# Six PSUM banks and exponentials of 1024 columns in the last two groups of an attention and experts kernel

## The reference

```python
scores = jnp.einsum('bsqhd,bthd->bqhst', qh, kh) * scale
probs = jax.nn.softmax(scores, axis=-1)
a_dot = jnp.einsum('bqhst,bthd->bsqhd', probs, vh)
...
a_mem = sigma_q @ memory / (sigma_q @ memory_norm)
out = a_dot * (1.0 - w) + a_mem * w
...
x = x + _L0_attn_ref(_layernorm(x))
x = x + _L0_ffn_ref(_layernorm(x))
```

## Time and profile before

| | us |
|---|---|
| median of 3 runs | 1948.24 |
| the three runs | 1952.13, 1948.24, 1946.98 |
| span of the profiled execution | 1946.1 |
| TensorE busy in it | 1871.1 (96%) |
| VectorE busy | 1030.1 (53%) |
| ScalarE busy | 980.6 (50%) |
| GpSimd busy | 921.2 (47%) |

### The profile page before, as it was taken

How to read it: one execution, slowest core, us unless ns; L and a number is a source line. 1 busy time by engine, 2 the same in 40 slices (tenths; PEclk the granted TensorE clock), 3 DMA queues, 4 the chain that set the end, 5 groups by cost and what they waited for, 6 DMA issues and landing times.

```text
span 1946.1 us, 34880 instructions
## 1 busy us (share of the span) xinstructions
PE 1871.1 (96%) x9240; PEld 963.5 (50%) x9241; DVE 1030.1 (53%) x1995; ACT 980.6 (50%) x1917; POOL 921.2 (47%) x1127
## 2 busy tenths in 40 slices
PE   6799999999999999999999999999999999999996
PEld 5444445444544454445333455555555555555553
DVE  5667777878788878877887152222211222222213
ACT  3366776777677766776776532222332233322330
POOL 3532566666666766674643550333333333333342
PEclk9899999999999999999999999999999999999998
DMA  6423233534353335333542797877777777777779
GB/s 193 117 62 85 70 94 125 155 99 107 125 156 99 105 127 155 98 95 117 145 153 86 256 342 232 183 141 141 142 142 143 142 141 141 143 144 141 142 165 260
DMA packets 159128, 277.71 MB, mean 143 GB/s; under 512 B 28704, under 2 KB 64800, under 8 KB 156256
## 3 DMA queue, kind: packets, MB, share of 16 engines
q1 hardware_dynamic: 108688, 147.61, 27.2%
q0 software_dynamic: 40880, 106.96, 26.8%
q10 hardware_dynamic: 9440, 21.68, 3.2%
HBM read 145.65 MB, written 135.74 MB: 145 GB/s over the span
## 4 chain that ended last, share of the span: by engine, by line
PE 83%; ACT 5%; DMA 4%; DVE 3%; issue 2%; POOL 1%; SPq 1%; DVEq 0%; POOLq 0%
PE ps_gu L1911 22%; PE ps_pv L1210 12%; PE ps_exp L1197 10%; PE ps_max L1183 9%; PE ps_y L1930 7%; PE ps_misc L1103 5%; PE ps_y L1934 4%; PE ps_x L1890 4%; ACT prob L723 3%; DVE mx L973 2%; PE ps_misc L1128 2%; PE ps_misc L1152 2%; DMA wts_sb<-second_sum_rows 1%; PE ps_misc L1223 1%; PE ps_misc L1074 1%
## 5 line engine op out<-in xcount | busy, mean ns | idle before, releaser
L973 DVE TENSOR_REDUCE mx<-ps_max 128x2 f32<-128x1024 f32 x512 | 617.6, 1219 | 169.5 <-PE ps_max L1183 155.4
L723 ACT ACTIVATE prob<-ps_exp 128x512 f32<-128x512 f32 x1024 | 584.0, 597 | 152.9 <-PE ps_exp L1197 135.2
L1197 PE MATMUL ps_exp<-qs,ks 98*128 98x512 bf16 x1024 | 391.3, 383 | 23.0 <-ACT prob L723 19.8
L1911 PE MATMUL ps_gu<-wts_sb,xT 128*128 x1152 | 402.7, 493 | 1.5 <-issue 1.5
L1610 POOL DMA_INDIRECT out<-yt,idx x72 | 111.7, 1551 | 468.4 <-ACT yt L1679 453.9
L1183 PE MATMUL ps_max<-ks,qs 96*128 96x512 bf16 x1024 | 308.0, 382 | 8.0 <-DVE mx L973 4.4
L1791 DVE COPY hT<-ps_h 128x384 f32<-128x384 f32 x88 | 49.0, 557 | 464.0 <-PE ps_h L1920 464.0
L1911 PEld LDWEIGHTS ps_gu<-wts_sb,xT 128*128 128x128 f32 x1152 | 207.3, 190 | 171.1 <-issue 56.7
L1210 PE MATMUL ps_pv<-prob,vs 128*32 128x512 f32 x2048 | 253.3, 608 | 0.0
L1669 ACT ACTIVATE gs<-ps_gu 128x192 f32<-128x192 f32 x176 | 58.2, 330 | 376.7 <-PE ps_gu L1911 376.7
L1197 PEld LDWEIGHTS ps_exp<-qs,ks 98*128 98x128 bf16 x1024 | 99.5, 97 | 209.2 <-ACT prob L723 99.7
(11 more groups left out here) (191 smaller groups left out, 2146.8 us busy)
## 6 DMA issues: line engine op xcount, KB each, us to landing
xt<-rows_by_expert SPq DMA_DIRECT2D x144, 264.5 KB, 2.7
dnr_sb<-in_dnr SPq DMA_DIRECT2D x144, 128.0 KB, 2.6
qk_parts<-parts POOLq DMA_DIRECT2D x112, 120.0 KB, 3.6
qs<-qk_parts SPq DMA_DIRECT2D x64, 192.0 KB, 3.1
wts_sb<-in_wts ACTq DMA_DIRECT2D x12, 1024.0 KB, 7.6
x_sb<-in_x SPq DMA_DIRECT2D x16, 512.0 KB, 4.6
qs<-qk_parts SPq DMA_DIRECT2D x64, 128.0 KB, 3.1
x_plus_memory<-am SPq DMA_DIRECT2D x16, 512.0 KB, 5.3
```

Of the source, the lines that this page charges most:

```text
L723: act.activation(prob[:, s, q], ps_exp[:, q % 2], ACT.Exp, scale=SCALE).then_inc(s_exp, 1)
L973: dve.tensor_reduce(mx[:, k % 2, 4 * s + 2 * p:4 * s + 2 * p + 2], ps_max[:, p], AX_X, ALU.max).then_inc(s_maxd, 1)
L1197: pe.matmul(ps_exp[:, q % 2], ks[0:ROWS + MROWS, kk, s * P:(s + 1) * P], qs[0:ROWS + MROWS, kk, q], start=True, stop=True).then_inc(s_sc, 1)
L1911: mm = pe.matmul(ps_gu[:, i, 0:2 * I], xT[:, i, d], w, start=(d == 0), stop=(d == DC - 1))
```

## The change

In groups 64 and 65 (`alone(g)`):

- the scores of one place, two matmuls of 512 columns, go into one of three pairs of banks in turn: `ps_max[:, 0]`, `ps_exp`, `ps_max[:, 1]` (`DRAIN`, `drain_bank`). A pair waits for the exponential three places before it; the first and the third of group 64 wait for VectorE's last maxima, the second for the last exponential of group 63.
- one ACTIVATE takes both, 1024 columns over two banks, and counts 2 on `s_exp`.
- TensorE makes the block t = 2, 3 of the head before at place 2 instead of 0, and the block t = 0, 1 at place 6 instead of 4; ScalarE copies oT behind the exponential of place 1 instead of 0.

```diff
+    def alone(g):
+        return NG <= g < NG + 2
+
+    DRAIN = [ps_max[:, 0], ps_exp[:, :], ps_max[:, 1]]
+
+    def drain_bank(g, p):
+        return DRAIN[(8 * (g - NG) + p) % 3]
...
+            def exps_alone(g, s, half_):
+
+                n = 16 * g + 4 * s + 2 * half_ - 32
+                act.wait_ge(s_sc, n + 2)
+                if half_ == 0:
+                    act.wait_ge(s_pv, 4 * g + s - 11)
+                act.activation(prob[:, s, 2 * half_:2 * half_ + 2], drain_bank(g, 2 * s + half_), ACT.Exp,
+                               scale=SCALE).then_inc(s_exp, 2)
...
-                        if runs(g, 2, NG + 2):
+                        if alone(g):
+                            exps_alone(g, s, half_)
+                        elif runs(g, 2, NG + 2):
                             exps(g, s, (2 * half_, 2 * half_ + 1))
                         at(8 * k + p - 0.5)
-                        if p == 0 and runs(g, 3, NG + 3):
+                        if p == (1 if alone(g) else 0) and runs(g, 3, NG + 3):
                             oT_out(g)
...
+            def scores_alone(g, k, p):
+
+                n = 16 * g + 2 * p - 32
+                at = 8 * (g - NG) + p
+                if at in (0, 2):
+                    pe.wait_ge(s_maxd, 8 * NG - 1 + at // 2)
+                else:
+                    pe.wait_ge(s_exp, n - 2 if at == 1 else n - 4)
+                if p == 0:
+                    pe.wait_ge(s_mrow[(k + 2) % 4], 16 * MROWS * ((g - 2) // 4 + 1))
+                for i in range(2):
+                    s, q = p // 2, 2 * (p % 2) + i
+                    pe.matmul(drain_bank(g, p)[:, i], ks[0:ROWS + MROWS, (k + 2) % 4, s * P:(s + 1) * P],
+                              qs[0:ROWS + MROWS, (k + 2) % 4, q], start=True, stop=True).then_inc(s_sc, 1)
...
-                        if p == 0 and runs(g, 3, NG + 3):
+                        if p == (2 if alone(g) else 0) and runs(g, 3, NG + 3):
                             pv(g - 1, (k + 1) % 4, 2, 4 * g - 10)
                             at(between_halves(8 * k))
                             pv(g - 1, (k + 1) % 4, 3, 4 * g - 9)
-                        if p == 4 and runs(g, 2, NG + 2):
+                        if p == (6 if alone(g) else 4) and runs(g, 2, NG + 2):
                             for t in (0, 1):
                                 pv(g, (k + 2) % 4, t, 4 * g - 8 + t)
```

More of the change, by code:

```diff
@@ L1230, in body @@
                         p = 2 * s + half_
-                        if runs(g, 2, NG + 2):
+                        if alone(g):
+                            scores_alone(g, k, p)
+                        elif runs(g, 2, NG + 2):
                             scores(g, k, s, (2 * half_,))
@@ L1234, in body @@
                             scores_for_max(g, k, s, half_)
-                        if runs(g, 2, NG + 2):
+                        if runs(g, 2, NG + 2) and not alone(g):
                             scores(g, k, s, (2 * half_ + 1,))
-                        if p == 0 and runs(g, 3, NG + 3):
+                        if p == (2 if alone(g) else 0) and runs(g, 3, NG + 3):
                             pv(g - 1, (k + 1) % 4, 2, 4 * g - 10)
```

## The result

| | before | changed |
|---|---|---|
| median of 21 runs each | 1948.92 us (1944.76 to 1952.13) | 1945.02 us (1940.34 to 1949.73) |
| ratio to before | | 0.9983, interval 0.9975 to 0.9990 |
| the profiled execution | 1946.1 us span | 1945.6 us span |
| start of the last maxima to the last transposition of outputs ("the drain" below) | 1064.33 to 1095.79: 31.46 us | 1071.16 to 1096.17: 25.01 us |

The kernel is faster by 3.3 us, 0.17%. 1941.2 us with a gain of 7.0 was forecast: the sign is right, and less than half of the size came. The two profiled spans, only 0.5 us apart, are one execution each; what they compare is sorted out first, by experiment.

The account below looks back on a forecast made before the run. TensorE and ScalarE taking turns, with only two scores ahead, were taken to bound groups 64 and 65. Their 30.2 us would become 23.2, and the 7.0 us gain off the median 1948.24 gives 1941.2 us; range 1938.0 to 1945.5.

Parts of the forecast that it names:

- g = 65: place 2's scores wait for place 7's exponential, 1077.8: Timeline of group 65: TensorE goes on at 1076.1, place 2's scores wait until 1077.8, the next block starts at 1078.4.
- Banks: Groups 64 and 65: three pairs of banks let TensorE run three places ahead, costing two waits on the last maxima.
- The wider exponential: ScalarE in groups 64 and 65: 1024 columns take 1.02 us, 0.92 from start to start, against 1.08 for two today.
- The products two places later: Groups 64 and 65: blocks run while ScalarE works on places 1 and 2; price 0.9 us once, plus a stall behind mT.
- Half clock for the second block of g = 64: TensorE in group 64: little work precedes this block, so half clock was taken, 3.1 us, going on at 1076.1.
- The drain's gain, 7.0: First block to last transposition of outputs in groups 64 and 65: 30.2 us becomes 23.2, a gain of 7.0 us.
- Does it arrive?: Behind 1096 us: the same engines start everything, so the gain carries through; TensorE's 0.42 us wait for xt at 1182.69 stays.
- rival 3: Behind 1096 us: the gain is lost in a longer wait for xt, leaving 0 to 1 us; chance 0.12.
- Ranks 5 us earlier: Rank matmuls at place 4 of group 64 come ahead of the second block, at 1071.5 instead of 1076.54.
- The sums: The forecast's arithmetic, including the range's upper end of 1945.5 us and rival 4's drain end at 1101.8.
- Rival 2: Groups 64 and 65: the wide exponential costs 1.08 us, or one more stall comes in group 64; gain 4.4; chance 0.18.
- Rival 4: Groups 64 and 65: TensorE never gets its full clock, so the drain ends 6.0 us later, 1954.2 us; chance 0.05.

Follow-up runs that it names:

- the old places: Changed kernel with the products and oT back at places 0 and 4: ratio 0.9983; the same with weights loaded one block earlier: 0.9955, drain 22.94 us.
- the early loads: Changed kernel with the weights of experts 2 and 3 loaded one block of projections earlier: ratio 0.9961, drain 22.93 us.
- the early mT: Changed kernel with max_T between the two products of the first block and mT ahead of oT on ScalarE: ratio 0.9959, drain 25.81 us.
- The narrow kernel: Changed kernel with weights loaded one block earlier and two exponentials of 512 columns in place of each of 1024: ratio 0.9973, drain 22.68 us.

## Why the prediction was wrong, step by step

- **The step that failed is the chain's entry "g = 65: place 2's scores wait for place 7's exponential, 1077.8".** It let places 0 and 1 of g = 65 start as soon as TensorE went on at 1076.1. They need the maxima rows of the last head, and the chain never followed mT on through SyncE and its DMAs, though the kernel's description names `mT_out` and its two DMAs. Before, the rows landed 2.5 us ahead of use, so no wait was in the view; the move used up a margin that a list of waits can't show. Price in the profiles: a wait of 2.0 to 2.5 us each time, 2.1 us of drain at like clock, plus the half clock that came behind it in two of three. The drains of the changed kernel are 25.0, 26.7 and 30.1 us; the forecast was 31.46 - 7.0 = 24.5. Without the wait the drain is 22.9 and the time falls by 7.6 us. That this is near the forecast's 7.0 is in part luck: the forecast had a shorter gain in the drain and no 3.1 us lost ahead of it.
- *Banks*: right. The place's rhythm became ScalarE's.
- *The wider exponential*: 1.02 forecast, 1.027 and 1.030 measured; 0.92 from start to start, 0.90 to 0.92 measured. But the step credited the width with most of what the banks give: the narrow one runs at 0.96 with them. The Trainium skill (ScalarE: Activation LUTs, What ACT_TABLE_LOAD costs) gives 1.04 us and, with its overlap, 0.95; the rows lie a little below both.
- *The products two places later*: the stalls forecast were there (mT 1.2, oT 1.18, ranks 0.5 instead of 0.9 us), but the benefit that the chain built on them was not seen: with six banks the old places have the same drain, 22.94 us.
- *Half clock for the second block of g = 64*: not seen in the first profile, where the whole drain ran at 1.00. It came one group later instead, at 1079.4 and 1079.7, behind a wait that the chain did not have. The reading under it, that each fall comes behind a stretch in which TensorE did little, does not hold for its own second example: in the stretch from 1062.00 TensorE is busy for 3.10 of 3.40 us.
- *The drain's gain, 7.0*: 6.45 in the first pair of profiles; by the means of two and three profiles 33.3 becomes 27.3, 6.0; with the stretch ahead of the drain, 5.0. The timed runs say 3.3, with an interval of 1.9 to 4.9.
- *Does it arrive?* As far as the scatter lets one see. Behind the last transposition it is 850.3 us to the end before and 849.4 after (853.3, and 852.7 and 849.0, in the other executions), so there is no sign of rival 3. The waits for xt did not grow in the first pair: 1.3 us in total near 1170 to 1183 before and 0.64 after:

```profile
1172.89 0.66 PE L1927 MATMUL ps_x<-identf,xt 128*128 128x128 f32 x4 [0.64 <-DMA xt<-xn_rows]
```

- *Ranks 5 us earlier*: right, +7.1 instead of +12.2 from the last maxima.
- *The sums* hold but for two slips that change nothing: 1948.24 - 4.4 + 1.5 is 1945.3 and not 1945.5, and rival 4's end is 1101.9.
- *Rival 2*, a smaller gain, is where the time landed, but by another mechanism: neither a dear exponential nor a stall in g = 64. *Rival 4*, TensorE at half clock: the drain's clock rose, from 0.84 to 1.00 in the first pair. The rule on cycling through banks (the Trainium skill, TensorE: Matmul & The Clock Gate, A second HAM failure mode: psum-queue depth-cycling) would have it swing; without the wait for the rows, all five kernels with six banks ran their drain, 21.9 to 22.9 us, without a fall; but so did the changed kernel once with the wait, and all six profiles had two falls ahead of the drain.

**What stays open.** The profiles differ by 5.0 us over both stretches, the timed runs by 3.3. Runs without a profile can't be split, and five profiled executions are few. What the runs do carry is their mean granted clock, and it moves with the time: of the changed kernel's 21 runs the eight at 0.985 and 0.986 took 1947.4 us on average, the eleven at 0.988 and above 1943.1. Why the clock falls ahead of the drain in some executions and in it in the others isn't known, and it can't be told whether the early loads favour the one. The kernel with the early mT still waited 2.27 us in its one profile, and its time was as good as that of the early loads; over both stretches so was its profile. That the wait for the rows costs the timed runs what the profiles show rests on two pairs of kernels: changed 0.9983, 0.9984 and 0.9979 against 0.9961 with the loads early, and old places 0.9983 against 0.9955. The narrow kernel, 0.9973 without the wait, lies between.

## What to carry to other kernels

Before an engine is brought forward by some microseconds, follow each thing it will need there back to its start, small DMAs too, and write down how early it lands today: a margin of 2.5 us is no row of any list of waits, and a change of 7 us turns it into the next wait. Keep small urgent transfers clear of megabytes issued just ahead. And take a change of several parts apart once it works: here one part carried all of the gain that the profiles can show. And before a short stretch is compared between two profiles, look at the clock ahead of it too.

## What the runs showed of the hardware

- Two DMAs of 4 KB from SyncE landed 5.8 to 8.0 us after their issue in three profiles with 2 MB of weights issued by POOL shortly before them (4 us before, in the changed kernel), 4.7 and 4.8 with 6.5 us between, and 1.6 to 3.2 us without, though they are another engine's. In eight profiles the second of them landed 1.3 to 3.2 us behind the second megabyte. I had taken such a hand-over as free.
- A wait of 2 to 2.5 us on TensorE was followed by 3.4 us at 1.2 GHz in two executions of the same kernel and not in a third. In fourteen profiles the six whose clock fell twice in the 90 us ahead of the drain kept the full clock in it, and the other eight did not. Over some 30 us of drain this scatter, 5 us, is as large as the effect studied.
- The start of the drain, 1064 to 1073 us, varies from one execution to the next by more than the whole gain, so two profiled spans can't be compared; the stretch between two named instructions can, with the clock beside it.
